# Normalised rows on ScalarE, and transposes laid two tiles to a bank, in a fused graph, attention and expert kernel

## The chip, the cores and the metric

The kernel runs on 1 core of one Trainium2 chip. The metric is the device time of one execution in microseconds (us). The engines of the core are named as the profile names them: PE (TensorE; PEld is its weight load), DVE (VectorE), ACT (ScalarE), POOL (GpSimd) and SP (SyncE, which issues DMAs here). Each takes its instructions in order, and they meet at semaphores.

## What is computed

x is 3125 rows of 256 fp32 numbers. Three parts are added up:

```
xn = layernorm(x)
graph: m = concat(h[src], edge_attr); tmp = relu(m @ W1.T + b1); h_N = segment_sum(tmp, dst)
       h_lin = relu(concat(h, h_N) @ W2.T); graph = h_lin / max(norm(h_lin), 1e-12)   (100000 edges)
mix, 4 layers:
       h = layernorm(x)*g + b; q = softmax(h @ Wq, in each head); k = softmax(h @ Wk, over the rows)
       context = k^T v (8 heads of 32); x = x + (q @ context) @ Wo + bo
       h = layernorm(x)*g + b; x = x + gelu(h @ W1 + b1) @ W2 + b2
x = x + graph(xn) + mix(xn)
x = x + layernorm(z + the two chosen of 16 experts of z),  z = layernorm(x)
```

## The kernel before, in words

The 3125 rows are 25 tiles of 125 rows (T), in 5 groups g of 5 tiles. For the four mix layers l all engines run one hand-written order; into it are woven the steps of the graph part, `step(n)`: a step is 500 edges. On PE a step is `pe_edges` (two products of `aT` with `Wst`, line 437, which wait for the DMA that brings `aT`) and the sums of the step before (lines 429 and 430); on POOL four gathers (line 875); on DVE `dve_edges`: `z` (line 477), the add into `agg` (457), the one-hot matrix (464) and `zl` (451); on ACT `zr` (445).

A layer begins with the **keys' phase**, the loop `for g in range(NG)` that stands once in each engine's program. The softmax of the keys goes over all rows, so it runs with a maximum that is corrected from piece to piece; a group has two pieces, tiles 0 to 2 and tiles 3 and 4 (`PC`), and two halves h of the 256 columns. For group g the order is:

- PE: keys of piece 0 (line 1310, both halves), a step, keys of piece 1 half 0, `context(g-1)` (line 1295: 20 matmuls that multiply the transposed exponentials `es` of the group before with its normalised rows `NORM[(g-1) % 2]`), keys of piece 1 half 1, a step, `normalised_T(g+1)` (line 1255: the rows of the next group, transposed), then the transposes of the exponentials `eT` (line 1326).
- DVE: the maxima of the keys (`reduce_max`, line 1760), the new maximum `nb` (1763) and its change `cdiff` (1765). Between the two maxima of piece 1 stand the step, the update of `ctxS` with piece 0 of the context (1738), `normalised` for tiles 0 to 2 of the next group (line 1611: (X - mean) times 1/std), and the update with piece 1. After `cdiff` come tiles 3 and 4 of `normalised`, then the next step.
- ACT: `corr` (1010) and the exponentials of a piece (1012), after piece 0 the step's `zr`; after piece 1 `first_norm` (line 939: scale and shift of the four transposed pieces), `zr` of the next step, and `copy_tile` (line 944), which brings the five transposes of the exponentials to `es`, a tile at a time.
- SP: the `aT` of the next group's steps (line 507) are issued behind the write of the transposed rows to `nT_d` (line 712), which waits for `first_norm`.

PSUM banks are handed out by number. RING is 3 banks: PE fills unit u (`ring(u)`, semaphore `ring_full`) once ACT has copied unit u-3 (`ring_act`). Before the change a transpose of exponentials or queries takes one unit per tile, in a bank of 512 numbers of which it fills 256 or 250. ROW is 2 banks that DVE empties (`row_full`, `row_dve`). The functions `ring_k`, `ring_h2`, `row_c` and others work out these numbers; `RP` is the pairing ((0, 2), (2, 3), (3, 5)) that the rows' products already use, and NRP is 3.

`inverse_std` (line 1654) makes 1/std of some groups for the next keys' phase; it runs once in layer 0, three times in the feed-forward phase of layers 0 to 2, and once behind group 0 in layers 1 to 3: 13 times. There, ACT's `deviations` stand just behind the copies to `es`.

The **feed-forward phase** of a layer (PE line 1373 up, 1245 down, ACT line 1054 gelu) has between the two products of group g the attention of group g+1: `queries_T` transposes the softmaxed queries `qe` (PE line 1271), ACT copies them to `QT` tile by tile (line 944), and `attention` (line 1277) multiplies `QT` with `M_s`. For group 0 this stands ahead of that phase.

Of the kernel before, what the change touches and what calls it, by code (L numbers as in the profile page):

```python
# [11 lines left out]
def build(nc, x, src, dst, edge_attr, gnn_W1, gnn_b1, gnn_W2,  # L12
# [56 lines left out]
    with ExitStack() as ctx:  # L69
# [12 lines left out]
        def sem(name):  # L82
# [48 lines left out]
        rstd_t = sb("rstd_t", [T, NT])  # L131
        st5b = sb("st5b", [T, GT, 6])
# [183 lines left out]
        a_stat, a_aggr, a_mv, a_std, a_rstd = (sem(n) for n in ("a_stat", "a_aggr", "a_mv", "a_std", "a_rstd"))  # L316
        b_stat, b_aggr, b_std, b_rstd = (sem(n) for n in ("b_stat", "b_aggr", "b_std", "b_rstd"))
        l_init, k_max, m_new, nb_done, cd_done, m_cp, corr_done = (sem(n) for n in (
            "l_init", "k_max", "m_new", "nb_done", "cd_done", "m_cp", "corr_done"))
# [29 lines left out]
        RING_GA = [4 + (LNU if g + 1 < NG else 0) + GT for g in range(NG)]  # L349
        RP = ((0, 2), (2, 3), (3, 5))  # L350
        NRP = len(RP)
        pair_of = lambda j: next(i for i, (a, b) in enumerate(RP) if a <= j < b)
        ROW_GA = 2
        RING_GP = [2 * NF + (GT + LNU if g + 1 < NG else 0) for g in range(NG)]
        QIN = [1 <= g < NG - 1 for g in range(NG)]
        ROW_GP = [NRP * (1 + (g + 1 < NG) + QIN[g]) for g in range(NG)]
        RING_MP, ROW_MP = 1 + GT + LNU, 3 * NRP + 1 + KD
# [46 lines left out]
        def ring_h2(l, g):  # L404
            return ring_qT(l, g) + GT
# [511 lines left out]
        def _(act):  # L917
# [56 lines left out]
            for l in range(L):  # L974
# [13 lines left out]

                def q_softmax(g):
                    act.wait_ge(row_dve, row_q(l, g) + NRP + 1)  # L990
                    act.activation(qe[:, :, :], qe[:, :, :], ACT.Exp, scale=SCALE).then_inc(q_exp, 1)
# [5 lines left out]
                def queries_T(g):  # L997
                    u = ring_qT(l, g)
                    for j in range(GT):
                        copy_tile(u + j, u + j - RING_A, QT[:, :, j * T:(j + 1) * T], T)  # L1000
# [5 lines left out]
                for g in range(NG):  # L1006
                    u0, q0 = ring_k(l, g), l * (2 * NG) + g * 2
                    for pc, (a, b) in enumerate(PC):
                        act.wait_ge(cd_done, q0 + pc + 1)
                        act.activation(corr[:, g % 2, pc, :], cdiff[:, pc, :], ACT.Exp).then_inc(corr_done, 1)  # L1010
                        for h in range(KD):
                            act.activation(eT[:, h, a * T:b * T], RING[(u0 + 2 * pc + h - RING_A) % 3][:, 0:(b - a) * T], ACT.Exp,
                                           bias=nb[:, pc, h:h + 1], scale=SCALE,
                                           accum_out=piece_sum[:, g % 2, pc, h:h + 1]).then_inc(ring_act, 1)
                        if pc == 0:
                            step(step_k(l, g))
                    if g == NG - 1:
                        step(step_k(l, g) + 1)
                    if g + 1 < NG:
                        act.wait_ge(nT_out, (l * NG + g) * 16)  # L1020
                        first_norm(u0 + 4, u0 + 4 - RING_A, to=NORM_T[(g + 1) % 2])
                        step(step_k(l, g) + 1)
                    for j in range(GT):
                        u = ring_k(l, g + 1) - GT + j
                        copy_tile(u, u - RING_A, es[:, j, :].rearrange("p (k n) -> p k n", k=KD), 128, T)
                    if g == 0 and l > 0:
                        deviations(NG - 2, NG, l * NG + NG)
                    if g == 0:
                        step(step_k(l, g) + 2)
# [109 lines left out]
        def _(pe):  # L1139
# [119 lines left out]
            for l in range(L):  # L1259
# [6 lines left out]
                def queries_T(g):  # L1266
                    pe.wait_ge(q_norm, l * NG + g + 1)
                    for j in range(GT):
                        to = ring(ring_qT(l, g) + j)
                        for k in range(KD):  # L1270
                            ins = pe.transpose(to[:, 128 * k:128 * k + T], qe[:, j, 128 * k:128 * k + 128], ident[0:T, 0:T])
                        ins.then_inc(ring_full, 1)
# [4 lines left out]
                def attention(g, units):  # L1277
                    for i in units:
                        pe.wait_ge(ring_act, ring_qT(l, g) + RP[i][1] + 1)
# [7 lines left out]
                def context(g):  # L1287
                    r0, uT = row_c(l, g), ring_k(l, g + 1) - GT
                    for pc, (a, b) in enumerate(PC):
                        to = row_of(r0 + pc)  # L1290
                        for h in range(KD):
                            for j in range(a, b):
                                if h == 0:
                                    pe.wait_ge(ring_act, uT + j + 2)
# [4 lines left out]
                for g in range(NG):  # L1299
                    u0, uT = ring_k(l, g), ring_k(l, g + 1) - GT  # L1300
# [223 lines left out]
        def _(dve):  # L1524
# [129 lines left out]
            def inverse_std(a, b, n):  # L1654
                dve.wait_ge(a_std, n)
                dve.reciprocal(rstd_t[:, a * GT:b * GT], stdA[:, a * GT:b * GT]).then_inc(a_rstd, 1)
                dve.wait_ge(a_rstd, n)
            A_STD = NG - 1

            for l in range(L):  # L1660
# [84 lines left out]
                for g in range(NG):  # L1745
                    u0, q0 = ring_k(l, g), l * (2 * NG) + g * 2
                    for pc, (a, b) in enumerate(PC):
                        for h in range(KD):
                            if pc == 1 and h == 0:
                                step(step_k(l, g))  # L1750
                            if pc == 1 and h == 1:
                                if g:
                                    context(g - 1, (0,))
                                if g + 1 < NG:
                                    normalised(g + 1, NORM[(g + 1) % 2], range(*PC[0]))
# [10 lines left out]
                    if g + 1 < NG:  # L1766
                        normalised(g + 1, NORM[(g + 1) % 2], range(*PC[1]))
# [275 lines left out]
```

## Time and profile before

| | us |
|---|---|
| median of three executions | 2347.41 |
| lowest, highest | 2334.14, 2352.9 |
| the profiled execution, its own time | 2339.37 |
| its span in the profile | 2337.6 |
| TensorE clock granted in it, mean | 0.935 |

A row of the trace's timeline is a start and a duration in us from the span's start, the engine, the line of the kernel, the operation, the tiles and their shape, how many instructions are merged in the row, and in brackets how long the engine had been idle ahead of it and what released it. A row of the groups by line ends with the busy time in us, the mean of one instruction in ns, and the idle time ahead. The profiled time is 1.8 us above the span, which is what lies around it.

### The profile page before, as it was taken

To read this page: it belongs to the slowest core of one execution; us is meant where nothing else is said; L and a number is where in the kernel's file an instruction comes from. 1 tells how busy PE (TensorE), PEld (TensorE's weight loads), DVE (VectorE), ACT (ScalarE), POOL (GpSimd) and SP (SyncE) were. 2 spreads that over 40 slices of the span, in tenths; PEclk is the share of its full clock that TensorE was granted. 3 is DMA by queue.
4 is the path that set the end of the run, shared out by engine and by line. 5 is a ranking of instruction groups with operands and counts; after the bars stand their busy time and mean duration, and the time that the engine had idled before them with its cause. 6 is when DMAs were issued, how large, how long until landed. Compare 5 with 4: busy or idle time off the path is not lost.

```text
span 2337.6 us, 31898 instructions
## 1 busy us (share of the span) xinstructions
PE 1962.4 (84%) x10094; PEld 1594.8 (68%) x10094; DVE 1463.9 (63%) x3291; ACT 910.5 (39%) x1964; POOL 1356.0 (58%) x1123
## 2 busy tenths in 40 slices
PE   2448889999888999988899999889999985899990
PEld 1326667778666777866678777668777775788880
DVE  4747686766778677676876777686666557311116
ACT  1224344443435444344444444444444231233330
POOL 4157386667647666775666667567666500566650
PEclk9759999999999999999999999999999986899995
DMA  8564243333533332353333335343333421899997
GB/s 213 177 169 114 76 103 85 83 72 81 148 102 96 86 81 73 80 154 103 90 88 86 73 73 145 106 107 93 77 78 76 117 77 44 261 304 302 301 269 169
DMA packets 275536, 294.06 MB, mean 126 GB/s; under 512 B 146715, under 2 KB 204126, under 8 KB 275390
## 3 DMA queue, kind: packets, MB, share of 16 engines
q0 software_dynamic: 127488, 134.76, 24.0%
q1 hardware_dynamic: 143790, 157.50, 22.6%
q8 instruction: 70, 1.15, 0.2%
q10 hardware_dynamic: 4112, 0.03, 0.1%
q14 instruction: 76, 0.62, 0.1%
HBM read 243.19 MB, written 47.87 MB: 125 GB/s over the span
## 4 chain that ended last, share of the span: by engine, by line
PE 54%; DVE 18%; DMA 9%; ACT 7%; issue 6%; POOL 3%; SPq 1%; DVEq 1%; POOLq 0%; ACTq 0%
PE bank L1245 23%; PE bank L1373 11%; DMA TTQ<-zn_d,slot_tok 3%; PE bank L429 3%; PE bank L430 3%; PE bank L437 3%; DVE zl L451 2%; PE bank L1485 2%; DVE z L477 2%; DMA aT<-attr_d 2%; PE bank L1493 2%; ACT zr L445 2%; PE bank L1295 2%; POOL G L875 1%; PE bank L1310 1%
## 5 line engine op out<-in xcount | busy, mean ns | idle before, releaser
L875 POOL DMA_INDIRECT G<-P_d,src_T x896 | 1134.0, 1266 | 649.8 <-DVE z L477 382.6
L445 ACT ACTIVATE zr<-z 125x512 fp32r<-125x512 f32 x448 | 266.9, 629 | 349.2 <-DVE z L477 305.6
L451 DVE SCALAR_TENSOR_TENSOR zl<-z,zr 125x512 fp32r<-125x512 f32 x448 | 289.9, 688 | 140.3 <-ACT zr L445 130.9
L477 DVE TENSOR_TENSOR z<-bank,G 125x512 f32<-125x512 f32 x448 | 289.4, 684 | 136.7 <-PE bank L437 68.1
L1373 PE MATMUL bank<-TT,W_s 128*128 128x250 f32 (+1 forms) x1280 | 361.6, 428 | 15.9 <-ACT hid L1054 15.9
L1245 PE MATMUL bank<-W_s,hid 128*125 128x256 f32 x1600 | 361.1, 379 | 2.2 <-ACT hid L1054 2.2
L1245 PEld LDWEIGHTS bank<-W_s,hid 128*125 128x125 f32 x1600 | 293.8, 188 | 46.0 <-ACT hid L1054 3.8
L1373 PEld LDWEIGHTS bank<-TT,W_s 128*128 128x128 f32 x1280 | 235.7, 190 | 112.4 <-ACT hid L1054 23.1
L429 PE MATMUL bank<-zr,onehot 125*125 125x256 f32 x896 | 269.2, 332 | 21.8 <-DVE zl L451 21.7
L1054 ACT ACTIVATE hid<-bank,b_s 128x375 f32<-128x375 f32 x320 | 163.3, 521 | 271.3 <-PE bank L1373 223.6
L430 PE MATMUL bank<-zl,onehot 125*125 125x256 f32 x896 | 229.2, 286 | 0.0
L429 PEld LDWEIGHTS bank<-zr,onehot 125*125 125x125 f32 x896 | 170.9, 191 | 48.3 <-DVE onehot L464 30.1
L437 PE MATMUL bank<-Wst,aT 128*125 128x512 bf16 x448 | 139.2, 390 | 60.4 <-DMA aT<-attr_d 54.3
L430 PEld LDWEIGHTS bank<-zl,onehot 125*125 125x125 f32 x896 | 171.9, 192 | 5.6
L464 DVE TENSOR_TENSOR onehot<-iota_n,dst_T 125x500 fp32r<-125x500 f32 x224 | 152.5, 681 | 0.0
L1688 DVE TENSOR_TENSOR X<-bank,X 125x512 f32<-125x512 f32 (+1 forms) x120 | 71.5, 598 | 107.3 <-PE bank L1245 94.6
L437 PEld LDWEIGHTS bank<-Wst,aT 128*125 128x125 bf16 x448 | 59.4, 139 | 93.4 <-issue 49.4
L939 ACT ACTIVATE TT<-bank,lnp 128x250 f32<-128x250 f32 (+1 forms) x128 | 67.9, 613 | 114.8 <-PE bank L1255 109.9
L1119 ACT ACTIVATE QT<-bank,b1e 128x128 f32<-128x128 f32 x256 | 73.2, 369 | 98.8 <-PE bank L1485 76.3
L895 POOL DMA_INDIRECT TTQ<-zn_d,slot_tok x32 | 31.5, 986 | 137.9 <-DVE slot_tok L1971 121.3
L1245 PE MATMUL bank<-M_s,QT 128*125 128x256 f32 x400 | 104.9, 414 | 2.1 <-DVE M_s L1793 2.1
L1245 PE MATMUL bank<-Wq_s,TTQ 128*125 128x256 f32 x400 | 96.2, 381 | 5.8 <-DVE qe L1671 5.8
(317 smaller groups left out, 2953.1 us busy)
## 6 DMA issues: line engine op xcount, KB each, us to landing
W_s<-in_L_ffn_w SPq DMA_DIRECT2D x64, 512.0 KB
hid<-in_L_ffn_w SPq DMA_DIRECT2D x64, 512.0 KB
G<-P_d,src_T POOLq DMA_INDIRECT x896
TTQ<-nT_d SPq DMA_DIRECT2D x20, 626.0 KB
W_s<-in_L_mix_W SPq DMA_DIRECT2D x8, 1024.0 KB
nT_d<-TT SPq DMA_DIRECT2D x12, 626.0 KB
aT<-attr_d SPq DMA_DIRECT2D x224, 31.2 KB
nT_d<-TTQ SPq DMA_DIRECT2D x8, 626.0 KB
```

Source lines behind the costliest of these rows:

```text
L429: nc.tensor.matmul(sum_bank[0:T, 0:D], onehot[:, s, i, :], zr[:, s, i // 2, cols], start=i == 0, stop=False)
L430: ins = nc.tensor.matmul(sum_bank[0:T, 0:D], onehot[:, s, i, :], zl[:, i // 2, cols], start=False, stop=i == ST - 1)
L437: nc.tensor.matmul(edge_bank[k][0:ET, :], aT[:, s, :], Wst[:, 2 * k * D:2 * (k + 1) * D], start=True, stop=True).then_inc(e_done, 1)
L445: nc.scalar.activation(zr[:, s, k, :], z[:, k, :], ACT.Relu).then_inc(r_done, 1)
L451: nc.vector.scalar_tensor_tensor(zl[:, k, :], z[:, k, :], 0.0, zr[:, s, k, :].bitcast(f32), ALU.max, ALU.subtract).then_inc(lo_done, 1)
L464: nc.vector.tensor_tensor(onehot[:, s, :, :], iota_n[0:ET, :].unsqueeze(1).to_broadcast([ET, ST, T]), dst_T[:, ds(e * ST, ST)].unsqueeze(2 ...
L477: nc.vector.tensor_tensor(z[:, k, :], edge_bank[k][0:ET, :], G[:, ST * s + 2 * k:ST * s + 2 * k + 2, :].rearrange("p j d -> p (j d)"), ALU ...
L875: pool.indirect_dma_start(G[:, j, :], None, P_d[:, :], bass.IndirectOffsetOnAxis(ap=src_T[:, at:at + 1], axis=0)).then_inc(g_in[j], 16)
L1054: act.activation(hid[:, f, a * T:b * T], RING[(u - RING_A) % 3][:, 0:(b - a) * T], ACT.Gelu, bias=b1_s[:, l * NF + f:l * NF + f + 1]).then ...
L1119: ins = act.activation(hT[s % 2][:, c, :], RING[1 + s % 2][:, c * SL:(c + 1) * SL], ACT.Relu, bias=b1e[s][:, c:c + 1])
L1245: ins = pe.matmul(to[0:T, (j - a) * D:(j - a) * D + D], w, m, start=n == 0, stop=n == len(pairs) - 1)
L1373: ins = pe.matmul(to[:, 0:(b - a) * T], W1_s[:, k, part], TT[:, k, TT_PIECES[pc]], start=k == 0, stop=k == KD - 1)
```

## The change

1. `normalised` for the keys' phase leaves DVE. ACT makes these rows (`first_rows`) as Identity with a scale 1/std and a bias -mean/std, two operands of one number per row. They stand behind the `zr` of the group's first step, ahead of the second `corr`: for groups g from 1 on tiles 0 to 2 wait for piece 0 of `context(g-1)`, tiles 3 and 4 for piece 1, since they overwrite the rows which that context reads. There are 4 groups times 5 tiles times 4 layers, 80 instructions.
2. For the bias, `inverse_std` gets one more small DVE instruction, `shift_t`, with a semaphore.
3. The transposes of exponentials and of queries go two, one and two tiles to a unit of RING: PE fills 512, 256, 512 columns (500, 250, 500 for the queries), and ACT empties each with one instruction in place of one per tile. The PE's waits follow the pairs; all transposes stay, 10 for each group.

```diff
@@ inverse_std (DVE)
                 dve.wait_ge(a_rstd, n)
+                dve.scalar_tensor_tensor(shift_t[:, a * GT:b * GT], mvA[:, a * GT:b * GT, 0], -1.0, rstd_t[:, a * GT:b * GT],
+                                         ALU.mult, ALU.mult).then_inc(a_shift, 1)
@@ keys' phase, DVE
                                 if g:
                                     context(g - 1, (0,))
-                                if g + 1 < NG:
-                                    normalised(g + 1, NORM[(g + 1) % 2], range(*PC[0]))
                                 if g:
                                     context(g - 1, (1,))
...
                     if g + 1 < NG:
-                        normalised(g + 1, NORM[(g + 1) % 2], range(*PC[1]))
                         step(step_k(l, g) + 1)
@@ keys' phase, ACT
+                def first_rows(g, js):
+                    for j in js:
+                        n = g * GT + j
+                        act.activation(NORM[g % 2][:, j, :], tile(X, n), ACT.Identity, bias=shift_t[:, n:n + 1],
+                                       scale=rstd_t[:, n:n + 1]).then_inc(hn_done, 1)
...
                         if pc == 0:
                             step(step_k(l, g))
+                            if g + 1 < NG:
+                                act.wait_ge(a_shift, max(l * (NG - 1) + (g >= 2), 1))
+                                for rows_pc in range(2):
+                                    act.wait_ge(row_full, row_c(l, g - 1) + rows_pc + 1 if g else row_k(l, 0))
+                                    first_rows(g + 1, range(*PC[rows_pc]))
...
-                    for j in range(GT):
-                        u = ring_k(l, g + 1) - GT + j
-                        copy_tile(u, u - RING_A, es[:, j, :].rearrange("p (k n) -> p k n", k=KD), 128, T)
+                    for i, (a, b) in enumerate(RP):
+                        u = ring_k(l, g + 1) - NRP + i
+                        act.wait_ge(ring_full, u + 1)
+                        act.activation(es[:, a:b, :].rearrange("p j d -> p (j d)"), RING[(u - RING_A) % 3][0:T, 0:(b - a) * D],
+                                       ACT.Copy).then_inc(ring_act, 1)
@@ queries_T, ACT
-                    for j in range(GT):
-                        copy_tile(u + j, u + j - RING_A, QT[:, :, j * T:(j + 1) * T], T)
+                    for i, (a, b) in enumerate(RP):
+                        act.wait_ge(ring_full, u + i + 1)
+                        act.activation(QT[:, :, a * T:b * T], RING[(u + i - RING_A) % 3][:, 0:KD * (b - a) * T].rearrange("p (k n) -> p k n", k=KD),
+                                       ACT.Copy).then_inc(ring_act, 1)
@@ queries_T, PE
-                    for j in range(GT):
-                        to = ring(ring_qT(l, g) + j)
+                    for i, (a, b) in enumerate(RP):
+                        to = ring(ring_qT(l, g) + i)
                         for k in range(KD):
-                            ins = pe.transpose(to[:, 128 * k:128 * k + T], qe[:, j, 128 * k:128 * k + 128], ident[0:T, 0:T])
+                            for j in range(a, b):
+                                at = (k * (b - a) + j - a) * T
+                                ins = pe.transpose(to[:, at:at + T], qe[:, j, 128 * k:128 * k + 128], ident[0:T, 0:T])
                         ins.then_inc(ring_full, 1)
@@ attention, PE
-                        pe.wait_ge(ring_act, ring_qT(l, g) + RP[i][1] + 1)
+                        pe.wait_ge(ring_act, ring_qT(l, g) + i + 2)
@@ transposes of the exponentials, PE
-                    for pc, (a, b) in enumerate(PC):
+                    for i, (a, b) in enumerate(RP):
+                        pe.wait_ge(ring_act, u0 + (3 if b <= PC[0][1] else 5))
+                        to = ring(uT + i)
                         for j in range(a, b):
-                            pe.wait_ge(ring_act, u0 + (2 * pc + 3))
-                            to = ring(uT + j)
                             for h in range(KD):
-                                ins = pe.transpose(to[0:T, 128 * h:128 * h + 128], eT[:, h, j * T:(j + 1) * T], ident[:, :])
-                            ins.then_inc(ring_full, 1)
+                                at = (j - a) * D + 128 * h
+                                ins = pe.transpose(to[0:T, at:at + 128], eT[:, h, j * T:(j + 1) * T], ident[:, :])
+                        ins.then_inc(ring_full, 1)
```

The numbering follows (GT becomes NRP in `RING_GA`, `RING_GP`, `RING_MP`, `ring_h2`, `context`), and two semaphores that nobody used are gone.

## Rows read from the trace of the kernel before

**Rows 1.** The page, part 1: busy time of each engine, share of the span, instructions.
```profile
PE 1962.4 (84%) x10094; PEld 1594.8 (68%) x10094; DVE 1463.9 (63%) x3291; ACT 910.5 (39%) x1964; POOL 1356.0 (58%) x1123
```

**Rows 2.** The page, part 4: the chain that ended last, shares by engine.
```profile
PE 54%; DVE 18%; DMA 9%; ACT 7%; issue 6%; POOL 3%; SPq 1%; DVEq 1%; POOLq 0%; ACTq 0%
```

**Rows 3.** Windows: busy PE, PEld, DVE, ACT, POOL, clock, DMA; the sum: four keys' phases.
```profile
594.00:700.00 106.00, 91.15 (x426) 69.24 (x425) 76.36 (x192) 46.48 (x120) 59.53 (x48) 0.94 0.47 131
...
sum 427.00, PE 362.19 PEld 278.40 DVE 307.77 ACT 184.60 POOL 241.90; mean PE 90.55 PEld 69.60 DVE 76.94 ACT 46.15 POOL 60.48
...
720.00:1010.00 290.00, 274.59 (x1365) 222.05 (x1366) 207.25 (x421) 131.67 (x233) 200.87 (x161) 0.99 0.34 83
```

**Rows 4.** Timeline, layer 1, group 3 of the keys' phase.
```profile
651.00 1.16 ACT L445 ACTIVATE zr<-z 125x512 fp32r<-125x512 f32 x2
...
652.04 1.69 ACT L944 ACTIVATE es<-bank 125x256 f32<-125x256 f32 x5
...
653.78 2.79 PE L1310 MATMUL bank<-TTQ,Wk_s 128*128 128x375 f32 x8 [0.47 <-ACT es L944]
...
656.42 0.19 PEld L437 LDWEIGHTS bank<-Wst,aT 128*125 128x125 bf16 x2 [0.46 <-DMA aT<-attr_d]
...
662.78 1.24 DVE L1611 TENSOR_SCALAR hn<-X,mvA,rstd_t 125x256 f32<-125x256 f32 x3
...
663.02 1.01 PE L1310 MATMUL bank<-TTQ,Wk_s 128*128 128x250 f32 x4
...
664.88 0.41 DVE L1760 TENSOR_REDUCE pm<-bank 128x1 f32<-128x250 f32 x1
...
665.71 0.20 ACT L1010 ACTIVATE corr<-cdiff 128x2 f32<-128x2 f32 x1 [5.56 <-DVE cdiff L1765]
```

**Rows 5.** Timeline, layer 1, end of group 1's keys; start of group 2's.
```profile
624.55 1.01 PE L1310 MATMUL bank<-TTQ,Wk_s 128*128 128x250 f32 x4
...
627.18 0.41 DVE L1760 TENSOR_REDUCE pm<-bank 128x1 f32<-128x250 f32 x1
...
634.25 4.63 PE L1310 MATMUL bank<-TT,Wk_s 128*128 128x375 f32 x8 [0.47 <-ACT es L944]
```

**Rows 6.** Timeline, layer 1, group 0.
```profile
606.01 0.41 DVE L1760 TENSOR_REDUCE pm<-bank 128x1 f32<-128x250 f32 x1
...
606.84 0.20 ACT L1010 ACTIVATE corr<-cdiff 128x2 f32<-128x2 f32 x1 [3.50 <-DVE cdiff L1765]
...
614.29 0.22 DVE L1656 RECIPROCAL rstd_t<-stdA 125x10 f32<-125x10 f32 x1 [2.42 <-issue]
```

**Rows 7.** The chain in order of time, layer 1, group 4: start, us, what.
```profile
669.70 7.20 DMA aT<-attr_d
```

**Rows 8.** Groups by line and form, whole span: busy us, mean ns, idle ahead.
```profile
L1611 DVE TENSOR_SCALAR hn<-X,mvA,rstd_t 125x256 f32<-125x256 f32 x125 | 47.5, 435 | 0.0
...
L1035 ACT ACTIVATE hid<-bank,lnp 128x256 f32<-128x256 f32 x8 | 4.1, 560 | 18.7 <-PE bank L1338 18.7
...
L953 ACT ACTIVATE X<-hn 125x256 f32<-125x256 f32 x25 | 10.5, 419 | 9.6 <-DVE hn L1611 9.6
...
L944 ACT ACTIVATE es<-bank 125x256 f32<-125x256 f32 x100 | 32.2, 394 | 4.9 <-PE bank L1326 3.2
...
L1079 ACT ACTIVATE QT<-bank 128x500 f32<-128x500 f32 x10 | 5.9, 592 | 44.1 <-PE bank L1404 44.1
...
L1763 DVE SCALAR_TENSOR_TENSOR nb<-pm,nb 128x2 f32<-128x2 f32 x40 | 6.4, 161 | 1.4
```

**Rows 9.** Timeline, layer 1, queries of group 1 in the feed-forward phase.
```profile
750.10 1.54 ACT L944 ACTIVATE QT<-bank 128x250 f32<-128x250 f32 x5
...
750.52 0.70 PE L1271 MATMUL bank<-ident,qe 125*128 125x125 f32 x4 [0.88 <-ACT QT L944]
...
751.06 2.75 PE L1245 MATMUL bank<-M_s,QT 128*125 128x256 f32 x12
```

**Rows 10.** Waits of PE from 700 to 1010 us: total, times, longest.
```profile
PE bank L1271 <- ACT QT L944: 4.7, 4, 1.3
```

More of the change, by code:

```diff
@@ L131, in build @@
         rstd_t = sb("rstd_t", [T, NT])
+        shift_t = sb("shift_t", [T, NT])
         st5b = sb("st5b", [T, GT, 6])
@@ L316, in build @@
         a_stat, a_aggr, a_mv, a_std, a_rstd = (sem(n) for n in ("a_stat", "a_aggr", "a_mv", "a_std", "a_rstd"))
+        a_shift = sem("a_shift")
         b_stat, b_aggr, b_std, b_rstd = (sem(n) for n in ("b_stat", "b_aggr", "b_std", "b_rstd"))
-        l_init, k_max, m_new, nb_done, cd_done, m_cp, corr_done = (sem(n) for n in (
-            "l_init", "k_max", "m_new", "nb_done", "cd_done", "m_cp", "corr_done"))
+        l_init, k_max, nb_done, cd_done, corr_done = (sem(n) for n in (
+            "l_init", "k_max", "nb_done", "cd_done", "corr_done"))
         cn_done, rk_done, key_summed = sem("cn_done"), sem("rk_done"), sem("key_summed")
@@ L348, in build @@
         LNU = 2 * KD
-        RING_GA = [4 + (LNU if g + 1 < NG else 0) + GT for g in range(NG)]
         RP = ((0, 2), (2, 3), (3, 5))
         NRP = len(RP)
+        RING_GA = [4 + (LNU if g + 1 < NG else 0) + NRP for g in range(NG)]
         pair_of = lambda j: next(i for i, (a, b) in enumerate(RP) if a <= j < b)
         ROW_GA = 2
-        RING_GP = [2 * NF + (GT + LNU if g + 1 < NG else 0) for g in range(NG)]
+        RING_GP = [2 * NF + (NRP + LNU if g + 1 < NG else 0) for g in range(NG)]
         QIN = [1 <= g < NG - 1 for g in range(NG)]
         ROW_GP = [NRP * (1 + (g + 1 < NG) + QIN[g]) for g in range(NG)]
-        RING_MP, ROW_MP = 1 + GT + LNU, 3 * NRP + 1 + KD
+        RING_MP, ROW_MP = 1 + NRP + LNU, 3 * NRP + 1 + KD
         RING_A, RING_L = NT, LNU + sum(RING_GA) + RING_MP + sum(RING_GP)
@@ L404, in ring_h2 @@
         def ring_h2(l, g):
-            return ring_qT(l, g) + GT
+            return ring_qT(l, g) + NRP
         def row_c(l, g):
@@ L1287, in context @@
                 def context(g):
-                    r0, uT = row_c(l, g), ring_k(l, g + 1) - GT
+                    r0, uT = row_c(l, g), ring_k(l, g + 1) - NRP
                     for pc, (a, b) in enumerate(PC):
@@ L1293, in context @@
                                 if h == 0:
-                                    pe.wait_ge(ring_act, uT + j + 2)
+                                    pe.wait_ge(ring_act, uT + pair_of(j) + 2)
                                 ins = pe.matmul(to[:, D * h:D * h + D], es[:, j, 128 * h:128 * h + 128], NORM[g % 2][:, j, :],
@@ L1299, in _ @@
                 for g in range(NG):
-                    u0, uT = ring_k(l, g), ring_k(l, g + 1) - GT
+                    u0, uT = ring_k(l, g), ring_k(l, g + 1) - NRP
                     pe.wait_ge(ring_act, u0 + 1)
```

## The prediction

> **What bounds the kernel now.** I begin with the page: PE is busy 84% of the span, DVE 63%, ACT 39% [rows 1], and the chain that ended last runs 54% on PE, 18% on DVE, 7% on ACT [rows 2]. So a saving on DVE or ACT counts only where their pieces stand in that chain, and the next view is the windows. The four keys' phases last 427 us together with PE busy for 362 and DVE for 308, and in layer 1 the granted clock is 0.94; a feed-forward phase of 290 us has PE busy for 275 at 0.99 [rows 3]. The reader is to see two kinds of stage: the keys' phase is a relay between PE, DVE and ACT with gaps on all three, the feed-forward phase is PE alone with short gaps.
>
> The timeline of one group of the keys' phase shows the relay [rows 4]. ACT ends the five copies to `es` at 652.04 + 1.69 = 653.73, and PE, idle until then, starts the keys at 653.78. The keys' last product ends at 663.02 + 1.01 = 664.03. DVE takes its maximum only at 664.88, because before it come two updates and, at 662.78, three normalised rows. ACT, idle for 5.56 us, gets `corr` at 665.71. From there exponentials, `first_norm`, `zr` and the copies follow without a gap of ACT to the next group's keys. So DVE from 662.78 to 665.7 and all of ACT behind it are on the path; ACT's 5.56 us ahead are free.
>
> **The rows that leave DVE.** In group 3 the three rows start at 662.78, last 1.24 with their overlap and delay what follows by about 1.1 us, DVE's next update being ready. Without them DVE would be ready for the maximum at 663.8, but PE ends its product only at 664.03; with 0.1 for the semaphore (PE starts 0.05 behind ACT's end) the maximum starts at 664.13, 0.75 earlier than 664.88 [rows 4]. So PE is late next. In group 1 PE ends at 624.55 + 1.01 = 625.56, and the maximum stands at 627.18 [rows 5]: 1.6 us of room, so the full 1.0 comes. For group 2 I take 0.9: where the clock falls ahead of it (keys in 4.63 us instead of 2.79) [rows 4, 5] it has more room, else it is as group 3. Group 0 has no context ahead; its second maximum at 606.01 [rows 6] moves by 1.0. Group 4 makes no rows. A layer gives 1.0 + 1.0 + 0.9 + 0.75 = 3.65, four layers **14.6 us**. The other two rows, behind `cdiff`, delay only the next `z`, whose `zr` on ACT waits behind `first_norm`: nothing.
>
> **The rows that come to ACT.** No row of before has this form. The nearest are Identity with scale and bias from PSUM, 560 ns, and copies of 256 numbers from SBUF, 419, and from PSUM, 394 [rows 8]. I take 560 + 25 = 585, starting each 0.07 before the last ends (five copies in 1.69 [rows 4] at 394 each), so 0.515. Lower end 419, the copy; upper end 760, the 592 of a copy of 500 columns [rows 8] plus the 166 by which 560 stands above 394. For groups 1 to 3 the last two rows start when PE has done piece 1 of the context, just ahead of the product at 663.02; they end 1.1 us later, near 664.2. The new `corr` comes at 665.71 - 0.75 = 664.96: covered by 0.7 us. Queued behind this wait are `corr`, the exponentials and all that follows, but `corr` needs a product that PE issues behind the same context, so the wait itself adds nothing. Group 0 is tighter: ACT has 3.50 us [rows 6], 2.5 after the gain, and five rows take 4 times 0.515 plus 0.585 = 2.6. I cost that at 0.1 a layer, 0.4 in all; at the upper end five rows take 3.5 and it is 1.0 a layer, 4 in all. PE's `normalised_T` stands behind the next step and does not wait. In groups 1 to 3 the cover is gone only with rows of over 0.9 us, since two of them have 1.8 us.
>
> A page speaks against this part. The 80 rows cost DVE 435 ns each [rows 8] and ACT by my estimate 585, so ScalarE works 12 us longer than VectorE is relieved of. The Trainium skill, ScalarE: Activation LUTs, Rules for kernel authors, gives adding and multiplying to VectorE, not ScalarE. By the rule the move loses those 12 us, by the trace they lie in ACT's idle time. This is a rival below.
>
> **The small instruction.** `shift_t` is 13 instructions of the kind that takes 161 ns [rows 8] plus a semaphore's turn; between 0.16 and 0.3 each. Ten lie in DVE's slack. Three stand at the end of group 0 of layers 1 to 3, where DVE has been idle 2.42 us for ACT's deviations, and the next `z` follows the reciprocal at 614.29 [rows 6]: 3 times 0.2 = **0.6 lost**.
>
> **The copies to es.** Five take 1.69 [rows 4]. Two of 512 numbers at about 600 (592 for 500) and one of 394 [rows 8], less two overlaps of 0.07, are 1.45: 0.24 saved ahead of the next keys. All ten transposes now end while ACT makes `zr` (651.00 + 1.16), so no copy waits for PE. But in group 3 `aT` landed at 656.42, when the first keys were nearly done (653.78 + 2.79) [rows 4]: keys that start earlier wait for that DMA, whose issue hangs on `first_norm` and does not move against it. In group 4 the chain holds 7.20 us of the same DMA [rows 7]. So I count the 0.24 at the ends of groups 0 and 1 only: **1.9 us**; the ends are nothing and 0.24 times 16 = 3.8.
>
> **The queries.** PE's last four transposes waited 0.88 us for ACT's first copy and ended at 751.06, where the attention starts. ACT's copies start at 750.10, behind `zr` [rows 9]. With two tiles to a bank nothing waits for a copy; the attention needs only the first pair, 592 ns [rows 8]: 750.10 + 0.59 + 0.04 = 750.73, which is 0.33 earlier. Group 0's queries stand behind `M_s` and give nothing; 4 groups in 4 layers give 5.3. In that phase PE waited for these copies 4.7 us in 4 groups [rows 10], but most of that stays as one wait ahead of the attention, since ACT is late and not the bank. Part comes back as later waits for gelu: I take **4 us**, between 1 and 5.3.
>
> **The sum.** 14.6 - 0.4 - 0.6 + 1.9 + 4 = 19.5, so 20 us. Against the profiled execution's own time of 2339.37 (span 2337.6 and 1.8 around it) this is 2319. That execution lies 8 us below the median of 2347.41; the four times known average 2343.5, and I put the level there: **2323 us**, 0.9% below. A measurement of this kernel can tell about 1% (23 us) from no change.
>
> **Rivals.**
> First, the clock gives more. Keys at the lower level cost 4.63 - 2.79 = 1.8 us [rows 4, 5]; five of the twelve starts of groups 2 to 4 in the four layers had it (the one at 634.25 is among them), all behind the stretch in which PE waits for ACT in pieces. That stretch gets about 1 us shorter. Without those five, and with as many such losses gone at group 0 and in the feed-forward phases, the gain is 20 + 18 = 38: 2305. For it speaks the clock of 0.94 against 0.99 [rows 3]; against it, that PE's wait ahead of the keys becomes one unbroken idle time of some 1.6 us, by my estimate.
>
> Second, the gain is taken up. If ScalarE is late by the 12 us that its rows cost more, or if PE and `aT` hold each group where DVE did, some 8 us are left: 2335. For it speaks group 3, where PE is only 0.85 behind DVE and the DMA is exact to 0.15; against it, group 1. The first half of this rival is what the rule of the Trainium skill, ScalarE: Activation LUTs, Rules for kernel authors, would come to.
>
> Third, slower. The lower clock is granted more often, since the gaps are now single long ones: ahead of the keys (1.6 us against 0.47 behind a short burst) and ahead of the attention (about 1.2). If each of the other seven key starts and all 16 attentions ran at 1.2 GHz, the loss would be 23 times 1.7 = 39: 2343.5 - 20 + 39 = 2362. It decides from 12 such stretches on. Against it: PE's idle time in all becomes less.
>
> **How the numbers follow.** Forecast 0.58 (gain 14 to 27 us), the clock's gift 0.14, taken up 0.19, slower 0.09. Faster by over 1% are the gift and four tenths of the forecast's own case, 0.14 + 0.24 = 0.38; slower by over 1% is about half of the third rival, 0.05; the rest, 0.57, lies within 1%. The range goes from 2303, the gift, to 2343, no gain, which holds the second rival and the spread of the executions of some 9 us to each side, and leaves out most of the third.
>
> **What would show it.** In the changed profile `hn` on ACT should be 80 instructions of 560 to 620 ns, covered: `corr` still released by `cdiff`, ACT's idle time ahead of it 2 to 3 us lower. DVE's second maximum of piece 1 should stand within 0.2 us of the end of PE's product in group 3. The keys' phases should sum to 410 us from 427, the waits of line 1271 for copies be gone, and PE wait longer for `aT`. Wrong would be `corr` that waits for ACT itself, keys' phases not shorter by 10 us, or a clock below 0.92 in them.

## The result and the profile after

The changed kernel took 2314.48 us (median of four executions, 2308.47 to 2319.54) against 2341.73 for the kernel before beside it: a ratio of 0.9901, with a 95% interval of 0.9874 to 0.9928. By the medians that is 27 us, by the ratio 23; below, too, the two ways can differ by 1 to 4 us. Each ratio is to the kernel before, measured beside the other. One of the ten executions of `query_banks` took 5068.31 us at a granted clock of 0.363 and is left out of its ratio. The profiled execution of the changed kernel took 2316.51 us, 22.9 less than the 2339.37 of before, where the sum had said 20. The sum came out; its terms did not.

First the page of the changed kernel: the engines (part 1) and the chain's shares (part 4).

```profile
PE 1936.4 (84%) x10094; PEld 1581.7 (68%) x10094; DVE 1443.2 (62%) x3224; ACT 942.0 (41%) x1964; POOL 1357.0 (59%) x1123
...
PE 58%; DVE 14%; DMA 12%; ACT 7%; issue 4%; POOL 2%; SPq 2%; DVEq 1%; POOLq 0%; ACTq 0%
```

Against [rows 1] ACT has 31.5 us more and DVE 20.7 less. In the chain DVE went from 18% to 14%, and DMA from 9% to 12% [rows 2]. PE's busy time fell by 26 us with as many instructions. The span's mean granted clock does not show why (0.935 before, 0.933 after); the starts of the keys, below, do for a good part.

Next the groups by line and form of the changed kernel, whole span.

```profile
L994 ACT ACTIVATE hn<-X,shift_t,rstd_t 125x256 f32<-125x256 f32 x80 | 42.3, 590 | 18.4 <-PE bank L1314 17.4
...
L439 PE MATMUL bank<-Wst,aT 128*125 128x512 bf16 x448 | 141.5, 396 | 75.8 <-DMA aT<-attr_d 68.0 <-DVE z L479 7.1
...
L1290 PE MATMUL bank<-ident,qe 125*128 125x125 f32 x200 | 29.2, 297 | 7.6 <-DVE qe L1703 7.6
...
L1262 PE MATMUL bank<-M_s,QT 128*125 128x256 f32 x400 | 97.9, 393 | 15.0 <-ACT QT L1009 12.9 <-DVE M_s L1812 2.1
```

A row on ScalarE takes 590 ns (estimate 585). The queries' transposes no longer wait for a copy [rows 10]; that wait is now one ahead of the attention, 12.9 us in 20 groups. And PE waits 68.0 us for `aT`; the same group of the kernel before says:

```profile
L437 PE MATMUL bank<-Wst,aT 128*125 128x512 bf16 x448 | 139.2, 390 | 60.4 <-DMA aT<-attr_d 54.3 <-DVE z L477 4.9 <-issue 0.4
```

The timeline of the changed kernel, layer 1, group 3, answers to [rows 4].

```profile
644.88 1.38 ACT L1041 ACTIVATE es<-bank 125x512 f32<-125x512 f32 x3
...
646.31 2.79 PE L1329 MATMUL bank<-TTQ,Wk_s 128*128 128x375 f32 x8 [1.52 <-ACT es L1041]
...
654.56 2.76 ACT L994 ACTIVATE hn<-X,shift_t,rstd_t 125x256 f32<-125x256 f32 x5 [1.88 <-PE bank L1314]
...
656.02 1.01 PE L1329 MATMUL bank<-TTQ,Wk_s 128*128 128x250 f32 x4
...
656.23 0.87 DVE L1760 SCALAR_TENSOR_TENSOR ctxS<-ctxS,corr,bank 128x256 f32<-128x256 f32 x2 [0.52 <-PE bank L1314]
...
657.09 0.41 DVE L1780 TENSOR_REDUCE pm<-bank 128x1 f32<-128x250 f32 x1
...
657.92 0.20 ACT L1020 ACTIVATE corr<-cdiff 128x2 f32<-128x2 f32 x1 [0.60 <-DVE cdiff L1785]
```

Here all is as the working said. The copies take 1.38 (1.45 worked out). PE's product ends at 657.03 and DVE takes its maximum at 657.09. The rows lie ahead of `corr`, which waits for `cdiff` and not for ScalarE: 0.60 us of slack is left.

Where the time went I read from the starts of `corr` in the timeline: it comes twice in a group, so 40 of them cut the span into halves of groups (first to second `corr`), steps between groups, and what lies between a layer's last and the next layer's first. A keys' phase here is the stretch from its first `corr` to its last, 340.6 us in four layers before; the 427 us of the prediction are windows that begin ahead of it and end behind it. All in us, sums over four layers; "low" counts, of the 12 steps to groups 2 to 4, those longer than the 9.57 us (9.25 with the banks of `es`) that they take with the keys in 2.79. In every longer one the eight products of the keys took 3.98 to 5.37 us at a granted clock of 0.50 to 0.69, in every other one 2.79 at 1.00. "Again" is a second profile.

| kernel | halves of groups 0 to 3 | half of group 4 | steps 0 to 1 | steps 1 to 4 | keys' phases | all behind them | low |
|---|---|---|---|---|---|---|---|
| before | 121.5 | 42.0 | 53.1 | 123.9 | 340.6 | 1816.6 | 5 |
| before, again | 121.7 | 32.4 | 53.2 | 135.3 | 342.6 | 1811.9 | 9 |
| changed | 109.9 | 48.7 | 60.8 | 112.8 | 332.2 | 1799.3 | 1 |
| changed, again | 109.0 | 49.3 | 59.5 | 111.1 | 328.9 | 1803.2 | 0 |
| rows only | 108.4 | 38.4 | 56.8 | 130.4 | 334.0 | 1814.8 | 7 |
| query banks only | 121.5 | 35.2 | 55.9 | 133.2 | 345.8 | 1801.8 | 9 |
| both banks, no rows | 122.4 | 41.1 | 55.0 | 116.1 | 334.6 | 1796.5 | 3 |
| changed, weights late | 113.1 | 41.5 | 52.0 | 121.4 | 328.1 | 1802.2 | 6 |
| changed, `aT` first | 110.1 | 29.7 | 58.6 | 114.7 | 313.1 | 1801.3 | 2 |
| the same, again | 109.8 | 31.0 | 57.4 | 111.0 | 309.2 | 1802.3 | 0 |
| changed, both orders | 114.0 | 31.8 | 52.2 | 114.3 | 312.3 | 1799.7 | 2 |
| banks, `aT` first | 121.7 | 32.4 | 52.9 | 112.7 | 319.7 | 1803.3 | 1 |
| before, `aT` first | 121.4 | 29.1 | 54.1 | 134.6 | 339.2 | 1816.5 | 9 |
| changed, no rows from layer 1 on | 110.1 | 47.4 | 55.4 | 112.4 | 325.4 | 1798.0 | 1 |

Of the 22.9 us the keys' phases gave 8.4 (forecast 16), and all behind them 17.3 (forecast 4); the stretch ahead of the first `corr` lost 2.7.

### The profile page after: what moved, and what is told of

Its sections match the earlier page's. It is cut to its first block, busy times and chain, and to the rows that moved or that the text cites. A ratio compares the mean times of both kernels' runs of the same rounds, so it can differ in the third digit from the quotient of the medians.

```text
span 2314.7 us, 31807 instructions
## 1 busy us (share of the span) xinstructions
PE 1936.4 (84%) x10094; PEld 1581.7 (68%) x10094; DVE 1443.2 (62%) x3224; ACT 942.0 (41%) x1964; POOL 1357.0 (59%) x1123
## 4 chain that ended last, share of the span: by engine, by line
PE 58%; DVE 14%; DMA 12%; ACT 7%; issue 4%; POOL 2%; SPq 2%; DVEq 1%; POOLq 0%; ACTq 0%
PE bank L1262 24%; PE bank L1393 11%; DMA aT<-attr_d 4%; PE bank L1314 4%; PE bank L431 4%; PE bank L432 3%; PE bank L439 3%; DMA TTQ<-zn_d,slot_tok 3%; PE bank L1505 2%; PE bank L1329 2%; PE bank L1513 2%; ACT zr L447 2%; DVE z L479 1%; DMA G<-P_d,src_T 1%; DMA TT<-zn_d,slot_tok 1%
## 5 line engine op out<-in xcount | busy, mean ns | idle before, releaser
L431 PE MATMUL bank<-zr,onehot 125*125 125x256 f32 x896 | 273.2, 336 | 20.7 <-DVE zl L453 20.5
L1262 PE MATMUL bank<-M_s,QT 128*125 128x256 f32 x400 | 97.9, 393 | 15.0 <-ACT QT L1009 12.9
```

The lines of the kernel that those rows point to most:

```text
L431: nc.tensor.matmul(sum_bank[0:T, 0:D], onehot[:, s, i, :], zr[:, s, i // 2, cols], start=i == 0, stop=False)
L1262: ins = pe.matmul(to[0:T, (j - a) * D:(j - a) * D + D], w, m, start=n == 0, stop=n == len(pairs) - 1)
```

## The experiments

**The parts alone.** `rows_only` is the kernel before with `first_rows` and `shift_t` and the old banks. `query_banks` is the kernel before with the two-tile banks for the queries. `banks_only` is the changed kernel with the rows back on DVE and without `shift_t`:

```diff
@@ keys' phase, ACT
-                            if g + 1 < NG:
-                                act.wait_ge(a_shift, max(l * (NG - 1) + (g >= 2), 1))
-                                for rows_pc in range(2):
-                                    act.wait_ge(row_full, row_c(l, g - 1) + rows_pc + 1 if g else row_k(l, 0))
-                                    first_rows(g + 1, range(*PC[rows_pc]))
@@ inverse_std (DVE)
-                dve.scalar_tensor_tensor(shift_t[:, a * GT:b * GT], mvA[:, a * GT:b * GT, 0], -1.0, rstd_t[:, a * GT:b * GT],
-                                         ALU.mult, ALU.mult).then_inc(a_shift, 1)
@@ keys' phase, DVE
+                                if g + 1 < NG:
+                                    normalised(g + 1, NORM[(g + 1) % 2], range(*PC[0]))
...
+                        normalised(g + 1, NORM[(g + 1) % 2], range(*PC[1]))
```

Expected of the rows alone:

> The kernel before with the normalised rows on ScalarE and shift_t, the transposes still one tile to a bank. By the prediction: faster by 14.6 - 0.4 - 0.6 = 13.6 us. By the rival formed from the trace after (the gain of group 0 is given back ahead of the aT DMA that stands behind the layer's weights, that of group 4's start behind the load to TTQ): only the 0.7 to 0.8 us of each of groups 1 to 3 is left, 2.2 us a layer, 9 us in all; idle time of PE ahead of the product with aT grows by 5 us or more.

Measured 2331.11 us, ratio 0.9964 (0.9942 to 0.9987): 8 us. The halves of groups 0 to 3 fell by 13 us as worked out, but this kernel, too, waits more for `aT` in the steps 0 to 1 (56.8 against 53.1) and has 7 low starts.

> The kernel after with the rows back on VectorE, so only the two tiles to a bank. By the prediction: faster by 1.9 + 4 = 6 us. By the rival (the feed-forward phases of the trace after are 4.2 us shorter in each layer, and this comes from this part and the clock that it keeps up): faster by 15 us or more. By a third theory (the clock's stretches fall by chance and differ from execution to execution): 5 to 8 us, with stretches at the lower clock in the feed-forward phases as many as before.

Measured 2315.21 us, ratio 0.9896 (0.9863 to 0.9929): as fast as the whole change.

> The kernel before with the queries' transposes alone two tiles to a bank; those of the exponentials stay one to a bank. By the prediction 4 us faster (1 to 5.3). By the rival that the clock in the feed-forward phase is kept up by this edit: 12 to 17 us faster. In both, the attention of groups 1 to 4 starts 0.25 to 0.35 us earlier behind ScalarE's first copy, and PE no longer waits inside the transposes.

Measured 2327.68 us, ratio 0.9947 (0.9925 to 0.9969): 12 us where 4 had been forecast, all behind the keys' phases (1801.8 against 1811.9 and 1816.6). The banks of `es` are the difference to `banks_only`, measured beside it, 12.5 us, where 1.9 had been forecast. The two profiles differ by 16.0: in the table the steps 1 to 4 fall by 17.1 (12 times 0.32 of it are the copies, the rest low starts), and group 4 takes back 5.9. Another 5.3 lie behind the keys' phases, where these banks have no instruction; that part has no cause here.

> The kernel before once more, for a second trace of it. If the stretches at the lower clock are chance, they stand at other places and in another number than in the first trace (ten in the feed-forward phases, eleven in the keys' phases), and the phases differ by 1.7 us for each. If they are set by the order of the work, they stand at the same instructions.

Measured once, 2337.95 us. The second trace shows the same kernel with 9 low starts instead of 5, and less wait in group 4 for it. Four of the first five recur at the same group of the same layer, so the places are neither fixed nor pure chance.

**Where the queries' 12 us are.** The copies are 0.3 us a group sooner, as worked out: `QT` to `QT` 60.8 before, 60.5 after, in the feed-forward phases. The rest is the clock. In the kernel before the attentions of groups 2 and 4 of layer 1 ran at the lower level of 1.2 GHz, the first 12 products in 4.44 and 4.38 us against the 2.75 of group 1 [rows 9]; the granted clock was 0.60 and 0.62 against 1.00:

```profile
811.84 4.44 PE L1245 MATMUL bank<-M_s,QT 128*125 128x256 f32 x12
...
935.11 4.38 PE L1245 MATMUL bank<-M_s,QT 128*125 128x256 f32 x12
```

The changed kernel, groups 1, 2 and 4 of layer 1, with the wait ahead:

```profile
744.00 2.86 PE L1262 MATMUL bank<-M_s,QT 128*125 128x256 f32 x12 [0.87 <-ACT QT L1009]
...
804.50 3.62 PE L1262 MATMUL bank<-M_s,QT 128*125 128x256 f32 x12 [0.43 <-ACT QT L1009]
...
926.32 2.85 PE L1262 MATMUL bank<-M_s,QT 128*125 128x256 f32 x12 [1.05 <-ACT QT L1009]
```

In both profiles of the kernel before, the time from the last `QT` to the next layer's `corr` is 82.8 to 83.0 us, and from the third to the fourth, in layers 0 to 2, 62.4 or more in five of six; with the query banks the first is 80.9 to 81.8 in each of ten profiles, and the second 60.5 to 61.3. So a loss of clock that came at almost the same two places is gone or smaller. The stretch between the fourth and the fifth gains nothing beyond the copies: 60.7 or 60.8 in seven of eight layers before, 60.5 to 61.4 with the banks, and 63 in two single cases. Between the queries of groups 0 and 1, which I had costed at nothing, 0.7 us a layer are gained in the first pair of profiles and 0.2 to 0.3 in the second pair and with the query banks alone.

**Which wait took the rows' gain.** The changed kernel and a variant that loads the feed-forward weights of layers 1 to 3 later:

```diff
@@ SP, keys' phase: the loads of W1 and W2 leave the start of the layer
                     attr_steps(at, step_k(l, g + 1))
+                    if l and g in (1, 2):
+                        weights_F(l, g - 1)
```

> The kernel after once more, on the chip of the next three. Every theory: 0.990 of before, and in the trace keys' phases of 82 to 84 us, 332 in all, with group 4 taking 12 us between its two corrs and PE waiting 60 us or more in all for aT.

Measured 2313.11 us, ratio 0.9893 (0.9867 to 0.9918).

> The kernel after; SyncE issues the loads of W1_s and W2_s of layers 1 to 3 behind the aT of groups 1 and 2 and no longer at the layer's start. If the aT of group 0's third step waits only behind these 2 MB, the time from group 0's last corr to group 1's first falls from 14.1 to 17.3 us to about 13.1 (what ScalarE's deviations leave), and the kernel gains 4 to 8 us on the one after. If that wait has another cause (the gathers, the write to nT_d) nothing changes.

Measured 2312.84 us, ratio 0.9902 (0.9877 to 0.9927): no gain. The steps 0 to 1 fell to 12.87 us in layers 1 to 3, as they should if the weights hold the DMA up. But the step 1 to 2 rose to 11.45 and 10.72, and the chain of that kernel in layer 2 shows the next in the row, gathers that POOL starts one behind the other:

```profile
1003.34 1.21 POOL G L885
1004.55 0.31 issue
...
1014.14 7.56 DMA G<-P_d,src_T
```

In the changed kernel the chain holds this instead, then PE starts, and its keys run at the lower level:

```profile
1006.03 12.95 DMA aT<-attr_d
```

```profile
1019.02 1.11 PE L439 MATMUL bank<-Wst,aT 128*125 128x512 bf16 x2 [3.27 <-DMA aT<-attr_d]
...
1021.64 4.12 PE L1329 MATMUL bank<-TTQ,Wk_s 128*128 128x375 f32 x8
```

The kernel with the weights late has the banks of `es` and yet six low starts, so these banks do not keep the clock up by themselves. The granted clock says where it fell. This is its start of group 2 in layer 1. The first row is the window of the transposes of the exponentials: its length, the busy time of PE, PEld, DVE, ACT and POOL, the granted clock, and the share and rate of the DMA. The second is the keys.

```profile
620.56:622.65 2.09, 2.09 (x10) 1.63 (x10) 1.30 (x3) 2.09 (x5) 1.73 (x2) 0.67 0.44 129
...
623.65 4.66 PE L1337 MATMUL bank<-TT,Wk_s 128*128 128x375 f32 x7 [1.01 <-ACT es L1049]
```

Here the clock had fallen before the keys, during the ten transposes (0.67). With the clock up they take 1.57 us in one burst; this is the changed kernel ahead of the keys at 646.31:

```profile
643.21 1.57 PE L1346 MATMUL bank<-ident,eT 128*125 128x128 f32 x10 [0.22 <-ACT TTQ L941]
```

In the kernel before the burst is broken by a wait for a copy. These are the starts at 634.25 (low, a granted clock of 0.62 in the burst) and at 653.78 (full) [rows 4, 5]:

```profile
630.38 1.66 PE L1326 MATMUL bank<-ident,eT 128*125 128x128 f32 x6 [0.21 <-ACT TT L939]
632.59 1.19 PE L1326 MATMUL bank<-ident,eT 128*125 128x128 f32 x4 [0.55 <-ACT es L944]
...
650.37 1.35 PE L1326 MATMUL bank<-ident,eT 128*125 128x128 f32 x6 [0.21 <-ACT TTQ L939]
652.58 0.73 PE L1326 MATMUL bank<-ident,eT 128*125 128x128 f32 x4 [0.85 <-ACT es L944]
```

So I sorted the 168 starts of groups 2 to 4 in the fourteen profiles by the clock of the ten transposes ahead of them. Without the banks of `es` it had already fallen in the burst in 29 of 60, with them in 5 of 108, and all 34 starts were low. Where it was at 1.00 in the burst, the start was low in 10 of 31 without the banks and in 11 of 103 with them. The banks help most in the burst that they mend; why the clock falls in one burst and not in the next, the runs do not show.

**Group 4.** SP issues the first two `aT` of group 4 behind the write of the transposed rows and the load that brings back those of group 0, 626 KB each. The edit puts them ahead of the load:

```diff
@@ SP, keys' phase
                     if g == NG - 2:
+                        attr_steps(at, at + 2)
+                        at += 2
                         sp.wait_ge(ring_full, ring_k(l, g) + 4)
                         sp.wait_ge(nT_out, (l * NG + NG - 1) * 16)
                         load_normalised_T(0)
```

> The kernel after; in the keys' phase SyncE issues the first two aT of group 4 ahead of the load of group 0's rows to TTQ. If group 4's wait is that DMA's place in the queue, the time between group 4's two corrs falls from 12 us to about 8 and the kernel gains up to 16 us on the one after, less what the queries of group 0 then wait for TTQ. If the queue is not what holds aT, or the queries take the wait over, it gains under 4 us.

Measured 2298.52 us, ratio 0.9832 (0.9807 to 0.9858): 14.6 us faster than the changed kernel beside it, and faster than both kernels. The half of group 4 fell from 49.3 to 29.7. SP's rows of the changed kernel, layer 1:

```profile
661.06 0.33 SPq L714 DMA_DIRECT2D nT_d<-TT  x1
661.49 0.38 SPq L717 DMA_DIRECT2D TTQ<-nT_d  x1
661.91 8.04 SPq L509 DMA_DIRECT2D aT<-attr_d  x3
```

PE in the same stretch of the changed kernel:

```profile
663.38 2.79 PE L1329 MATMUL bank<-TT,Wk_s 128*128 128x375 f32 x8 [1.52 <-ACT es L1041]
668.95 0.65 PE L439 MATMUL bank<-Wst,aT 128*125 128x512 bf16 x2 [2.79 <-DMA aT<-attr_d]
...
669.75 0.41 PE L431 MATMUL bank<-zr,onehot 125*125 125x256 f32 x1
...
671.03 1.87 PE L1329 MATMUL bank<-TT,Wk_s 128*128 128x250 f32 x4
```

The kernel before:

```profile
671.49 4.48 PE L1310 MATMUL bank<-TT,Wk_s 128*128 128x375 f32 x8 [0.47 <-ACT es L944]
676.94 0.65 PE L437 MATMUL bank<-Wst,aT 128*125 128x512 bf16 x2 [0.98 <-DMA aT<-attr_d]
...
677.66 0.28 PE L429 MATMUL bank<-zr,onehot 125*125 125x256 f32 x1
...
678.38 1.01 PE L1310 MATMUL bank<-TT,Wk_s 128*128 128x250 f32 x4
```

The reader is to see three things. From issue to PE it is 668.95 - 661.91 = 7.04 us after, and 676.94 - 669.70 = 7.24 before [rows 7]: the DMA takes what it takes. The keys ended 1.7 us sooner at the full clock, and PE only waited longer. And behind the longer wait the clock fell: 0.41 for 0.28 a product, 1.87 for 1.01. In the two profiles of the changed kernel that last product was slow in eight of eight layers (1.14 to 1.87), behind waits of 2.62 to 3.79 us. In the two of before it was slow in one of eight, behind a wait of 3.52. The length of the wait does not settle it: in layer 2, before and in `banks_only`, the product ran at the full clock behind waits of 2.87 and 3.44. The first two rows are the kernel before, the others `banks_only`:

```profile
1092.99 0.65 PE L437 MATMUL bank<-Wst,aT 128*125 128x512 bf16 x2 [2.87 <-DMA aT<-attr_d]
1094.41 1.01 PE L1310 MATMUL bank<-TT,Wk_s 128*128 128x250 f32 x4
...
1079.99 0.65 PE L439 MATMUL bank<-Wst,aT 128*125 128x512 bf16 x2 [3.44 <-DMA aT<-attr_d]
1081.42 1.01 PE L1324 MATMUL bank<-TT,Wk_s 128*128 128x250 f32 x4
```

From group 3's second `corr` to group 4's, four layers take 82.0 and 80.1 us before, 85.8 and 86.3 after. So in group 4 the change loses 4 to 6 us. The nine profiles with the old order of the queue show it inside each kernel, too: the half of group 4 took 7.27 to 9.22 us behind 14 of the 15 low starts of that group (11.26 behind the other) and 9.74 to 14.15 behind all 21 at the full clock. Waiting for `aT`, PE loses what a full clock gained it in the keys of group 4. The Trainium skill, DMA: Bandwidth & Descriptors, section "Queues, rings and completion order", says that each DMA engine consumes the descriptors of one ring in order; these 31 KB behind twice 626 KB agree: the write landed at 665.71, the load at 668.19 and `aT` at 668.91.

With the edit, the same rows of the second profile of that kernel:

```profile
651.91 0.33 SPq L714 DMA_DIRECT2D nT_d<-TT  x1
652.28 1.53 SPq L509 DMA_DIRECT2D aT<-attr_d  x2
653.91 0.50 SPq L717 DMA_DIRECT2D TTQ<-nT_d  x1
```

```profile
656.91 0.65 PE L439 MATMUL bank<-Wst,aT 128*125 128x512 bf16 x2
...
658.33 1.01 PE L1331 MATMUL bank<-TT,Wk_s 128*128 128x250 f32 x4
```

`aT` lands 4.59 us behind its issue, 0.17 behind the write, PE does not wait for it, and the clock stays up.

> Both of these orders on the kernel after. If the two DMA waits are what took back the gain of the rows: 15 to 24 us faster than the kernel after, 0.980 to 0.984 of before, keys' phases of 78 us each. If PE or VectorE is right behind them: less than the sum of the two alone.

Measured 2298.49 us, ratio 0.9836 (0.9809 to 0.9863): the weights' order adds nothing to this one either.

**Are the rows worth anything?** Three kernels, measured side by side.

> The changed kernel with the first two aT of group 4 issued ahead of the load of the transposed rows, run again beside its relatives. Both theories expect what the first run gave: 0.983 of the kernel before, about 2298 us, keys' phases of 77 to 80 us from the first corr to the last.

Measured 2296.09 us, ratio 0.9839 (0.9816 to 0.9862).

> The banks alone (rows on VectorE), with the same two aT of group 4 issued early. My theory: the banks alone were as fast as the whole change because the rows' gain was used up in waits for aT in groups 0 and 4. Without the wait of group 4 that gain is seen: this kernel is 6 to 12 us behind the one with rows on ScalarE and the same order of DMAs, about 2306, its keys' phases 80 to 82 us instead of 77 to 80. The rival: with the keys at the full clock the rows cost nothing on VectorE either, since PE or ScalarE ends last: then the two are within 3 us.

Measured 2305.61 us, ratio 0.9869 (0.9850 to 0.9888): 9.5 us behind by the medians, 7 by the ratios, whose intervals just touch; the profiles show it more clearly, with keys' phases of 319.7 us against 313.1 and 309.2. That is as my theory said. With group 4's wait gone the rows' gain is seen; with it there, it was not. On the banks alone the order of the DMAs is worth 6 us by the ratios of two measurements apart (0.9896 and 0.9869), and their intervals overlap.

> The kernel before with the two aT of group 4 issued early and nothing else. My theory: the wait for aT of group 4 was there before the change too (7.20 us of DMA in the chain) and costs some 2 us a layer there, less than the 14.6 it costs the changed kernel, because VectorE and the lower clock held group 4 as well: 4 to 9 us faster than before, about 2330. The rival, that the order of the DMAs is worth the same whatever the rest: 14 to 15 us, 2322.

Measured 2331.19 us, ratio 0.9987 (0.9973 to 1.0): 3 us or nothing, less than the 4 to 9 I had expected, though far from the rival's 14. The same edit is worth 3 us in the kernel before, 14.6 in the changed one. The low starts say why: here and in the second profile of before all four starts of group 4 were low, so `aT` was nearly there when PE wanted it.

**Does ScalarE pay for the rows?**

```diff
@@ first_rows, ACT
+                        if l:
+                            act.sem_inc(hn_done, 1)
+                            continue
                         act.activation(NORM[g % 2][:, j, :], ...
```

> The changed kernel that makes the keys' phase's rows in layer 0 only; in layers 1 to 3 ScalarE counts the semaphore in their place, so 60 activations are left out and the context there is made from old rows. My theory: the rows lie in ScalarE's idle time except for about 0.1 us in group 0 of each layer, so this gains at most 1 us in all. The rival, by which work on ScalarE costs what it takes longer than on VectorE (60 times 0.155) or its whole time: 9 to 30 us faster, about 2305 or less.

Measured 2306.14 us, ratio 0.9873 (0.9854 to 0.9891), so some 5 to 6 us faster than the changed kernel by its ratios at other times (0.9893 and 0.9901); the intervals overlap. That is more than my theory's 1 us and less than the rival's 9, though the time itself is only 1 us above the 2305 that the rival had named: the run does not decide between them. The profile says where the time went. The halves of groups 0 to 3, where the rows stand, do not differ (110.1 against 109.9 and 109.0; group 0 alone 20.4 in all three), so the 60 rows are covered there. The difference in the table lies mainly in the steps 0 to 1 (55.4 against 60.8 and 59.5), in the wait for an `aT` that in layer 2 was issued at 1006.03, ahead of the phase's first `corr` at 1006.72 and so ahead of all rows. Whether the rows lengthen that wait in another way, or it was short by chance, stays open.

## Why the prediction came out, and where it did not

**The rows that leave DVE, 14.6 less 0.4.** The mechanism was right: halves shorter by 12 to 13 us in four layers, the maximum 0.06 us behind the end of PE's product in group 3, `corr` still released by `cdiff` in groups 1 to 3. Groups 1 to 3 gave 7.7 together, not 10.6. The 0.4 for group 0 did not show: the rows end 0.07 us ahead of its `corr`, and its halves take 20.4 us in four layers with the rows and without them. What failed is that these were taken as gains to the end. The 1.0 of group 0 is never seen: its half and the step behind it together take 77.2 us in four layers with the rows on DVE and 77.8 with them on ScalarE (both with `aT` first), since the step ends with an `aT` behind the weights. And in the change as it is, group 4 gave back 4 to 6 us. Alone the rows were worth 8 us, on top of the banks nothing that the intervals show, and 7 to 9.5 once group 4's `aT` came early. I had the 7.20 us of this DMA in [rows 7] and used them against the copies to `es` alone, not against what a keys' phase with a higher clock would run into.

**The rows on ScalarE.** 590 ns for 585, and no wait for ScalarE in groups 1 to 3. The 25 ns that the working put on top of the row of 560 had no row behind them; the measured row stands 30 above it. The Trainium skill, ScalarE: Activation LUTs, section "What ACT_TABLE_LOAD costs", gives 186 ns, 93 for each operand of one number per partition and 0.833 per element, which is 585 for this form; the trace agrees with 590. It gives an overlap of 93 ns between neighbours; here it is 92 to 96 ns within a piece. The five rows of group 3 take 2.76 us because ACT stands 0.08 us between the pieces, where it waits for the next part of the context, and those of group 0, without that pause, take 2.55. The working's 0.07, which it read from five copies in one row of the timeline, was an average over such a pause. The rule of the Trainium skill, ScalarE: Activation LUTs, section "Rules for kernel authors", that adds and multiplies go to VectorE, the first half of the second rival, is not borne out: 80 rows cost ScalarE 12 us more than they cost VectorE, and the halves in which they stand got shorter.

**The copies to es, 1.9.** Mis-sized. The copies gave 0.32 a group (9.57 to 9.25) instead of 0.24. But the banks of `es` brought 12.5 us, in the main because the low starts fell: 5 to 9 of 12 in each of five profiles without them, 0 to 3 in eight with them, 6 in the ninth, where the weights are late. Of the 39 without them 29 had fallen in the broken burst of transposes. A low one makes its step 1.4 to 3.0 us longer; in group 4 the shorter wait for `aT` gives that back. That was my first rival's mechanism with the third's reason turned round: I held PE's single longer wait ahead of the keys (0.47 to 1.52 us) to be what might lower the clock, and it came with a higher one.

**The queries, 4.** Mis-sized too: 0.3 a group as worked out, 10 us by the medians and 12 by the ratio, with the attentions that had stood at the lower level.

**The small instruction, 0.6,** is too small for these runs to show.

**The sum.** Two terms were too small by about 18 us, and the rows too large by some 14, since their gain ended in a DMA's wait. By the forecast's own test, keys' phases not shorter by 10 us, the working was wrong at that place (8.4 and, in the second pair, 13.7); that 20 us came out all the same is luck, two errors that cancel. The second rival's second half, the gain taken up by `aT`, and the first, the clock's gift, both came true at once. The third did not.

## What to carry to other kernels

Before a saving is counted in a loop over stages, follow it to the stage with the longest DMA wait and ask whether its landing moves along: if it is set by an issue behind large transfers, the saving only lengthens the wait, and the first edit to try is the order of the queue. Parts of a change are not additive where they meet in one wait: the same two lines in the queue's order were worth 14.6 us in one version of this kernel and 3 and 6 in two others, the last two hardly clear of noise. And a short busy-idle-busy stretch of PE that recurs at the same place should be read for its clock in two profiles, since merging its small waits was worth more here than the waits.

## What was not expected of the hardware

PE's clock held at 2.4 GHz behind one idle stretch of 1.52 us more often than behind a burst of transposes with waits and 0.47 us: 16 low starts of 108 against 39 of 60, and in 29 of those 39 it was down already in the burst. Behind waits of 2.6 to 3.8 us for `aT` it fell in eight of eight layers of the changed kernel, but not behind 2.87 before and 3.44 in `banks_only`. Only the granted clock and the durations show this; what decides it was not measured. The number of low starts also differed between two executions of the same kernel, 5 and 9, at spans of 2337.6 and 2336.2 us; the one with more of them waited 10 us less in group 4.
